# Latent attention: the item scores over three PSUM banks with one exponential per head, four banks for the maxima, and the maxima's transposes ahead of a step instead of inside it

## The reference, cut to what matters

```python
latent = layernorm(x @ Wdkv.T, ln_g, ln_b)          # 1024 x 128
k, v = latent @ Wuk.T, latent @ Wuv.T               # 16 heads of 16
q, k = apply_rope(q), apply_rope(k)
scores = einsum('bhqd,bhkd->bhqk', q, k) / sqrt(16)
scores = where(causal, scores, -inf)
attn = softmax(scores, axis=-1)
out = einsum('bhqk,bhkd->bhqd', attn, v) @ Wo.T
```

## Time and profile before

| | us |
|---|---|
| median of 3 runs (2764.66 to 2770.92) | 2766.2 |
| the profiled execution | 2761.74 |
| its span in the profile | 2760.0 |
| PE busy | 2590.6 (94%) |
| DVE busy | 1391.6 (50%) |
| ACT busy | 1043.6 (38%) |
| latent loop of the second batch item | about 1048 to 1204 |

### The profile page before, as it was taken

How to read it: one execution, slowest core, us unless ns; L and a number is a source line. 1 busy time by engine, 2 the same in 40 slices (tenths; PEclk the granted TensorE clock), 3 DMA queues, 4 the chain that set the end, 5 groups by cost and what they waited for, 6 DMA issues and landing times.

```text
span 2760.0 us, 43707 instructions
## 1 busy us (share of the span) xinstructions
PE 2590.6 (94%) x16830; PEld 1637.8 (59%) x16831; DVE 1391.6 (50%) x3834; ACT 1043.6 (38%) x1964; POOL 312.2 (11%) x436
## 2 busy tenths in 40 slices
PE   7999999999999999998999999999999899969998
PEld 4555674454565664455555664465556664448997
DVE  3443376753333477743333577733433576743443
ACT  3444133443444234433443224434443224422121
POOL 2000010212000010211000011221000011222111
PEclk9999999998999999999999999999999999989999
DMA  3000000001000000001000000001000000042111
GB/s 103 12 12 1 16 1 1 2 14 43 12 12 1 16 1 1 2 18 39 18 7 1 16 1 2 2 29 33 12 7 1 16 1 1 2 163 70 51 57 37
DMA packets 33487, 57.28 MB, mean 21 GB/s; under 512 B 7915, under 2 KB 24504, under 8 KB 32920
## 3 DMA queue, kind: packets, MB, share of 16 engines
q1 hardware_dynamic: 28552, 41.73, 4.8%
q0 software_dynamic: 4752, 13.02, 1.3%
HBM read 40.41 MB, written 14.32 MB: 20 GB/s over the span
## 4 chain that ended last, share of the span: by engine, by line
PE 88%; ACT 4%; DVE 3%; issue 3%; POOL 1%; another core or an unknown queue 0%; DMA 0%; DVEq 0%; POOLq 0%
PE ps L958 10%; PE ps L1179 9%; PE ps L930 9%; PE ps L903 8%; PE ps L1213 7%; PE ps L1231 6%; PE ps L888 6%; PE ps L948 5%; PE ps L1306 5%; PE ps L1320 4%; PE ps L913 4%; PE ps L843 3%; PE ps L859 2%; PE ps L1079 1%; PE ps L1063 1%
## 5 line engine op out<-in xcount | busy, mean ns | idle before, releaser
L1408 DVE TENSOR_REDUCE neg_max<-ps 128x1 f32<-128x128 f32 (+7 forms) x256 | 194.0, 758 | 593.4 <-PE ps L933 547.9
L1179 PE MATMUL ps<-arena 32*128 32x512 f32 (+3 forms) x1536 | 449.3, 534 | 11.3 <-DVE arena L1615 6.7
L796 ACT ACTIVATE arena<-ps 128x1024 f32<-128x1024 f32 (+1 forms) x320 | 299.8, 938 | 373.9 <-PE ps L1213 373.8
L1213 PE MATMUL ps<-arena 32*128 32x256 f32 (+1 forms) x2560 | 368.7, 392 | 0.0
L930 PE MATMUL ps<-arena 128*128 128x512 f32 (+3 forms) x768 | 304.1, 508 | 22.2 <-ACT arena L736 17.5
L958 PE MATMUL ps<-arena 128*128 128x512 f32 (+3 forms) x768 | 318.8, 502 | 5.2 <-ACT arena L727 1.4
L727 ACT ACTIVATE arena<-ps 128x512 f32<-128x512 f32 (+3 forms) x384 | 187.9, 490 | 296.0 <-PE ps L948 294.0
L1213 PEld LDWEIGHTS ps<-arena 32*128 32x128 f32 x2560 | 213.8, 185 | 117.0 <-issue 99.5
L930 PEld LDWEIGHTS ps<-arena 128*128 128x128 f32 x768 | 143.7, 197 | 160.3 <-issue 127.3
L903 PE MATMUL ps<-turned_t,arena 128*128 128x512 f32 x512 | 228.9, 600 | 1.1 <-ACT turned_t L698 1.1
L1179 PEld LDWEIGHTS ps<-arena 32*128 32x128 f32 x1536 | 171.6, 187 | 68.7 <-DVE arena L1615 27.0
(11 more groups left out here) (218 smaller groups left out, 3575.4 us busy)
## 6 DMA issues: line engine op xcount, KB each, us to landing
arena<-in_w_qkv SPq DMA_DIRECT2D x32, 384.0 KB, 3.1
arena<-in_w SPq DMA_DIRECT2D x2, 4096.0 KB, 16.7
xin<-in_x SPq DMA_DIRECT2D x5, 1024.0 KB, 5.4
xres_ids<-sorted_res SPq DMA_DIRECT2D x35, 129.0 KB, 2.2
xin<-sorted_rows SPq DMA_DIRECT2D x35, 128.0 KB
w_out<-in_w_out SPq DMA_DIRECT2D x1, 1024.0 KB
out<-xin,out_row POOLq DMA_INDIRECT x35, 2.8
sorted_res<-xin SPq DMA_DIRECT2D x4, 129.0 KB
```

The lines of the kernel that those rows point to most:

```text
L796: nc.scalar.activation(mprobs_t[n % BUFS][:, 2 * pair:2 * pair + 2, 0:QUARTER + more], ps[:, bank:bank + 2, 0:QUARTER + more], ACT.Exp).th ...
L1179: last = nc.tensor.matmul(ps[:, MAX_BANK[m], at:at + n], q_heads_t[rows_j, g, t * P:(t + 1) * P], k_heads_t[rows_j, g, c * BANK:c * BANK + ...
L1213: last = nc.tensor.matmul(ps[:, 3 + j, kb * QUARTER:kb * QUARTER + n_q], k_heads_t[rows_j, g, keys_at:keys_at + P], q_heads_t[rows_j, g, ( ...
L1408: nc.vector.tensor_reduce(neg_max[:, par, t:t + 1], ps[:, buf:buf + 2, :].rearrange("p a n -> p (a n)")[:, 0:n], AX.X, ALU.max, negate=Tru ...
```

## The change

Each of the four heads of an item gets its own exponential and its own semaphore step: `mst_done` and `mexp_done` count heads. The head numbered 4n+j takes bank 3 + (4n+j) mod 3, so banks 3, 4 and 5 are used in turn, and a head's first block waits for the exponential of the head three before. Bank 6 goes to the maxima, whose chunks now use 0, 1, 2, 6. In a step the order is: first block of a, the two chunks, first block of b, second block of a, second block of b. The transposes of the maxima (TURN_LEAD 4 for 3) stand at the head of a step, behind the value products of the step before.

```diff
-TURN_LEAD, TAKE_LEAD = 3, 4
+TURN_LEAD, TAKE_LEAD = 4, 4
 WIDE = 12
+CHUNK_BANKS = (0, 1, 2, 6)
...
-        bank = m % 7 if m < WIDE else m % 3
+        bank = m % 7 if m < WIDE else CHUNK_BANKS[m % 4]
...
+ITEM_BANKS = 3
+
+
+def item_bank(n, j):
+    return 3 + (GROUP * n + j) % ITEM_BANKS
...
-                    pool.wait_ge(mexp_done, b * (2 * ITEMS) + 2 * n + 2)
+                    pool.wait_ge(mexp_done, b * (GROUP * ITEMS) + GROUP * n + GROUP)
...
-                    for pair in range(2):
-                        bank = 3 + 2 * pair
-                        act.wait_ge(mst_done, b * (2 * ITEMS) + 2 * n + pair + 1)
-                        nc.scalar.activation(mprobs_t[n % BUFS][:, 2 * pair:2 * pair + 2, 0:QUARTER + more],
-                                             ps[:, bank:bank + 2, 0:QUARTER + more], ACT.Exp).then_inc(mexp_done, 1)
+                    for j in range(GROUP):
+                        act.wait_ge(mst_done, b * (GROUP * ITEMS) + GROUP * n + j + 1)
+                        nc.scalar.activation(mprobs_t[n % BUFS][:, j, 0:QUARTER + more],
+                                             ps[:, item_bank(n, j), 0:QUARTER + more], ACT.Exp).then_inc(mexp_done, 1)
...
                 def item_scores(n, pair, first, end):
 
                     u, g, q, p, more = item_of(n)
+                    for v in range(len(UNITS)):
+                        if first < end and first == turn_at(v, TURN_LEAD):
+                            turn_max(v)
                     if p == 0 and pair == 0:
                         pe.wait_ge(ms_taken, b * MAX_SLOTS + turn_count(u, TAKE_LEAD) + 1)
-                    if n >= 1:
-                        pe.wait_ge(mexp_done, b * (2 * ITEMS) + 2 * n - 1 + pair)
...
+                    def bank_free(j):
+
+                        if GROUP * n + j >= ITEM_BANKS:
+                            pe.wait_ge(mexp_done, b * (GROUP * ITEMS) + GROUP * n + j - ITEM_BANKS + 1)
+
+                    j0, j1 = 2 * pair, 2 * pair + 1
+                    bank_free(j0)
+                    block(j0, 0)
+                    for s in range(first, end):
+                        max_chunk(s)
+                    bank_free(j1)
+                    block(j1, 0)
+                    block(j0, 1).then_inc(mst_done, 1)
+                    block(j1, 1).then_inc(mst_done, 1)
```

More of the change, by code:

```diff
@@ L1203, in item_scores, with block @@
                     u, g, q, p, more = item_of(n)
+                    for v in range(len(UNITS)):
+                        if first < end and first == turn_at(v, TURN_LEAD):
+                            turn_max(v)
                     if p == 0 and pair == 0:
                         pe.wait_ge(ms_taken, b * MAX_SLOTS + turn_count(u, TAKE_LEAD) + 1)
-                    if n >= 1:
-                        pe.wait_ge(mexp_done, b * (2 * ITEMS) + 2 * n - 1 + pair)
-                    for kb in range(2):
+                    def block(j, kb):
                         n_q = (QUARTER, more)[kb]
[L1210 to L1218, removed]
+                        rows_j = slice(SLOT * j, SLOT * (j + 1))
+                        keys_at = (2 * p + kb) * P
+                        return nc.tensor.matmul(ps[:, item_bank(n, j), kb * QUARTER:kb * QUARTER + n_q],
+                                                k_heads_t[rows_j, g, keys_at:keys_at + P],
+                                                q_heads_t[rows_j, g, (q + 1) * QUARTER - n_q:(q + 1) * QUARTER], start=True, stop=True)
+                    def bank_free(j):
[10 more added lines that the diff above has]
+                    block(j1, 1).then_inc(mst_done, 1)
                 def item_products(n, kb):
@@ L1227, in item_products @@
                             pe.wait_ge(mdiag_done, b * len(UNITS) + u + 1)
-                        pe.wait_ge(mexp_done, b * (2 * ITEMS) + 2 * n + 2)
+                        pe.wait_ge(mexp_done, b * (GROUP * ITEMS) + GROUP * n + GROUP)
                     n_q = (QUARTER, more)[kb]
```

## The result

| | before | after |
|---|---|---|
| median, us (4 runs each) | 2767.86 | 2691.28 |
| ratio, 95% interval | | 0.9723 (0.970 to 0.9745) |
| span of the profiled execution, us | 2760.0 | 2684.1 |

The kernel became 2.8% faster, 77 us, twice what was forecast and outside the range. These ratios have intervals of about 0.5% either way, so the readings rest on the traces, where at the full clock the same 20 steps repeat within 0.02 us from one batch item to the next, and from one profile of the kernel after to the other.

The account below looks back on a forecast made before the run. TensorE, busy 94%, was taken as the bound, its loop steps stretched by chunk waits and transposes. Gains less b's wait and edges gave 9.6 us a batch item, 38 for four: 2728 us, 8 in 10 within 2700 to 2756.

Parts of the forecast that it names:

- transposes at the head: Loop steps with transposes: 0.37 us per pair without a drain, 1.5 us in 20 steps for 4.4.
- floor of a step: Attention loop: a step without waits takes 1.63 us, a head's two blocks plus the products; 32.6 us in 20 steps.
- what was forecast: Loop's three runs of 20 steps: 36.3 us each for 39.88, a gain of 3.6, three times 10.7 us.
- b's wait: b's first block waits for the exponential three heads before: 0.14 us a step on average, 2.2 us in 20 steps.
- row statistics: Middle run of the loop: VectorE's row statistics don't fit into the slack, so its 1.4 us of excess stays.
- end of the loop and allowance: 11 steps without chunks cost 1.5 us, the last exponentials 0.2, moments with VectorE further behind 0.5.
- ahead of the loop: Stall of a chunk waiting for `take_max`, since transposes had taken one of three banks, goes: 1.1 us gained.
- the three banks: Second chunk waits about 0.3 us for VectorE to free its bank; four banks remove 2.9 us in 20 steps.
- Rival C: In steps with chunks, b starts only behind the chunks' second parts, 0.54 us later: slower, 2830 us; chance 0.08.
- Rival B: The exponential comes later, so b's mean wait is larger: 2747 us at 0.22, no gain at 0.30; chance 0.15.
- Rival D: b's wait in the loop is hidden, a's exponential being ready 0.3 us earlier: 2695 us; chance 0.07.
- The clock: Half-speed stretches outside the loop may be met otherwise by a shifted program: less than 10 us either way, not priced.

Follow-up runs that it names:

- e5_floor: e1_turns with the chunks inside the loop cut to 8 columns on TensorE and VectorE; 20 steps 32.15 us at the full clock, whole kernel 2910.9 us.
- e4_inside: The kernel after with the transposes inside the step again, behind its first chunk (lead 3); 20 steps 38.28 us, median 2694.77 us, ratio to before 0.985.
- e1_turns: The kernel before with only the transposes moved to the head of a step; 20 steps 35.59 us, median 2669.66 us against 2734.17.
- e3_three: The kernel after with three banks for the maxima, bank 6 unused in the loop; 20 steps 36.3 us, median 2695.90 us, ratio to before 0.986.
- e10_chunks_last: The kernel after with b's first block ahead of the two chunks again; 20 steps 36.96 us, ratio to before 0.984.
- e9_bias: The kernel after with a per-row bias operand of zeros in each exponential; 20 steps 35.9 us, ratio to before 0.980.
- after_again: The kernel after, unedited, run again in a later group; 20 steps 35.02 us, median 2661.00 us against 2725.74, ratio 0.9752.

## Why the prediction was wrong

The sign was right; the size was half. The mechanisms were found where the prediction put them: no chunk waits for its bank in ordinary steps, b waits for the exponential, and transposes at the head cost 0.37 us. What was wrong is the floor from which all of it was counted. The gain term by term, for one batch item at the full clock (the first four rows split the 15.6 us that the 60 steps gained in the second):

| term | forecast, us | measured, us |
|---|---|---|
| 60 steps: floor of a step (1.63 against 1.53) | 0 | +5.7 |
| 60 steps: what was forecast, which the other rows correct | +10.7 | +10.7 |
| b's wait, 2.2 against 2.9 in 20 steps | (in the row above) | -1.9 |
| excess of the run with row statistics | 0 | +1.1 |
| first steps of the loop | 0 | +0.8 |
| end of the loop and allowance | -2.2 | -0.9 |
| ahead of the loop | +1.1 | +2.0 |
| sum | 9.6 | 17.5 |

**The step that failed** is "1.63 is the floor of a step". It was read from two steps with value products of 256 columns and laid on all 20. The steps with 128-column products, and those whose scores are cut by the causal mask, are shorter, down to 1.42. A floor that is too high does not change how long the steps take now (39.88 was measured), so it enters the forecast in full: the excess to be removed was 39.88 - 30.7 = 9.2 us in 20 steps, not 7.3. e5_floor measures it: its steps take 1.63, 1.47 or 1.42 us, and 0.37 more with transposes.

Step by step, the 9.2 us lie as follows. The four steps with transposes (10.95 us in all) are 4.75 above their own floors, not 4.4; at the head the pairs cost 1.5, so their place is worth 3.3, which is what e4_inside shows with four banks. The other steps of the kernel before are 4.5 above theirs, not 2.9, and 2.0 of this is in the four right behind the transposes (1.98 to 2.23 us), where the second chunk starts only 0.44 to 0.55 us into the step, later than the 0.34 of the earlier trace rows. The prediction put all of it down to the three banks. In e1_turns, still with three banks, the excess of the steps other than the pairs' own 1.5 us is 3.4: about 1.0 us of waiting on chunks went with the transposes, which makes their place worth 4.3 there.

**b's wait** had the right cause: b starts 1.92 us after the step before it (1052.00 to 1053.92), as the prediction's 1.27 + 0.60 + 0.05 gives. Its mean was forecast for steps of 1.63; shorter steps leave the exponential less time, and the four waits above 0.3 us all stand behind value products of 128 columns. So the waits grow, to 35.02 - 32.15 = 2.9 us in 20 steps for 2.2. That figure takes in all that the chunks still cost. The exponential of 512 columns was taken at 0.60 and measured at 0.595. The Trainium skill, ScalarE: Activation LUTs, section "Rules for kernel authors", budgets 0.3 us of fixed part for an activation with a bias operand; the runs show 683 ns for 512 columns with one (0.26 of fixed part at 0.83 ns an element) and 595 without (0.17).

**The row statistics** were left in the forecast with their 1.4 us. With four banks 0.25 us of them remain, so the slack of two steps takes in most of VectorE's extra work, which the prediction held to be too much for it; with three banks they cost 1.9 to 2.2 (e1_turns, e3_three).

**Rival C** (b only behind the chunks' second parts) did not happen: b's first part starts at 1053.92, ahead of the chunks' second parts at 1054.19, though the chunks stand before it in the program. The Trainium skill, TensorE: Matmul & The Clock Gate, section "The mechanism", has matmuls start strictly in program order; the trace agrees if a matmul starts with its first part: the first parts of a, of the chunks and of b start in program order (1053.65, 1053.66, 1053.92). What b overtakes are the second parts, and these the prediction took for starts; so the rule does not make the case of rival C for fp32 matmuls in two parts. Their ends are reported in order, as the page says, and e10_chunks_last shows what that costs. **Rival B** priced a later exponential rightly in kind (e9_bias), but it did not occur. **Rival D**, whose 2695 is nearest to the result, came out by the number and not by its mechanism: b's wait is there.

**The clock** brought the rest, inside the 10 us that the prediction allowed it. 17.5 x 4 is 70; the spans differ by 75.9, although what lies outside the loops and the stretches ahead of them became 1.5 longer. In the profile before, the first five steps of the fourth loop and parts of three stretches ahead of a loop had less than the full clock:

```profile
2250.90:2272.76 21.86, 19.81 (x84) 7.90 (x84) 13.39 (x46) 2.52 (x5) 0.00 (x0) 0.93 0.00 1
2272.76:2293.21 20.45, 20.19 (x151) 12.29 (x150) 11.88 (x36) 7.61 (x9) 2.20 (x2) 0.66 0.00 1
1047.62:1063.04 15.42, 14.57 (x151) 8.40 (x150) 11.58 (x36) 7.50 (x9) 2.20 (x2) 1.00 0.00 1
```

The same five steps take 20.45 us with a mean granted clock of 0.66 and 15.42 with 1.00. The kernel after had its one such stretch in these places ahead of the fourth loop (21.53 us for 18.29). Together this is 6.8 us of the difference. Whether the change caused it is open: after_again, the same program in a later group of runs, had none of its stretches ahead of the loops below 19.9 us.

## What to carry to other kernels

A floor read from one step must be read from each kind of step in the loop; measure it by emptying the work that is thought to be hidden, since an error in it goes into the forecast in full. Work that needs another tiling of the array belongs where the array is drained anyway: moving two small transposes there was worth more than the exchange of banks. Where a queue is in order, put what does not wait ahead of what does, also because completion is reported in program order: the same wait cost 1.9 us more in 20 steps when it stood in front of the chunks.

## What the runs showed of the hardware

The clock can stay at its lower level through a whole loop in which TensorE is hardly ever idle (busy for 227.6 of 227.7 us in the second batch item). e5_floor runs the same loop four times. In the first batch item the granted clock is 1.00 (2.4 GHz) and 20 steps take 32.15 us. In the second it was at 0.50 (1.2 GHz) when the loop began, in the third and the fourth it fell some 3 us into the loop, and in all three it stayed there to the end of the loop: 20 steps take 57.76 us, 1.80 times as long, with PE busy for all 57.76. The fall in the third loop, in windows (its loop begins at 1688.05):

```profile
1679.00:1688.05 9.05, 9.05 (x30) 2.89 (x28) 5.91 (x13) 0.00 (x0) 0.00 (x0) 1.00 0.00 0
1688.05:1691.20 3.15, 3.00 (x41) 2.69 (x42) 2.58 (x19) 1.37 (x2) 0.00 (x0) 1.00 0.00 0
1691.20:1706.50 15.30, 15.30 (x113) 8.42 (x111) 2.67 (x23) 6.14 (x8) 2.20 (x2) 0.50 0.01 2
```

Ahead of the fall TensorE was busy for 12.05 of 12.20 us, first with the chunks ahead of the loop and then with the first steps. Only the work of the chunks is missing against e1_turns, which had 1.00 in every run of 20 steps whose windows are used here. Less work on TensorE made the whole kernel 2910.9 us long. What exactly decides whether the clock rises again is not settled by these runs.

Between the column-tiled value products and the row-tiled scores behind them the profile shows no idle time of TensorE, and yet the next score block starts 0.57 us after value products of 256 columns and 0.36 after those of 128 (1053.08 to 1053.65, 1056.68 to 1057.04). The difference is 128 columns fewer in each of a product's two parts (a head's parts stand 0.21 us apart for 256 columns, 1102.05 to 1102.27 in the earlier trace rows, so 0.11 for 128). How much of the distance is due to the change of tiling, and how much to the products themselves, no run here separates.
